# Two attention layers on a graph: one byte plane for two granules of the adjacency matrix, and one spill a block

## The reference, cut to what matters

```python
def layer0(h, adj, a):                       # N = 4096, D = 64
    src, dst = h @ a[:D, 0], h @ a[D:, 0]
    e = src[:, None] + dst[None, :]
    e = where(e > 0, e, 0.01 * e)
    e = where(adj > 0, e, -9e15)
    return softmax(e, axis=1) @ h
def layer1(x, adj, w, a, bias):
    wh = x @ w
    e = leaky_relu((wh @ a[:D, 0])[:, None] + (wh @ a[D:, 0])[None, :], 0.01)
    return softmax(where(adj > 0, e, -1e9), axis=1) @ wh + bias
x = layernorm(x + layer0(x, adj, a0))
x = layernorm(x + layer1(x, adj, w1, a1, bias1))
```

## Time and profile before

| | us |
|---|---|
| median of 3 runs | 499.06 (497.96 to 500.22) |
| the profiled execution | 498.63 |
| its span, first to last instruction | 496.9 |
| PE busy | 446.2 (90%) |
| PEld busy | 415.6 (84%) |
| DVE busy | 410.8 (83%) |
| ACT busy | 395.6 (80%) |
| POOL busy | 87.2 (18%) |
| VectorE, 32 x `to_bytes` | 74.1, 2315 ns each |
| HBM read / written | 77.74 MB / 9.44 MB |

### The profile page before, as it was taken

One profiled execution on the slowest core, in us unless ns is written; L12 is line 12 of the kernel. 1 busy time (PEld: TensorE's weight loads), 2 busy tenths in 40 slices (PEclk: granted clock), 3 DMA queues, 4 the chain that ended last, 5 costly groups with the idle time before them and its releaser, 6 DMA issues.

```text
span 496.9 us, 11765 instructions
## 1 busy us (share of the span) xinstructions
PE 446.2 (90%) x4420; PEld 415.6 (84%) x4420; DVE 410.8 (83%) x742; ACT 395.6 (80%) x589; POOL 87.2 (18%) x61
## 2 busy tenths in 40 slices
PE   0799768988989899998898969999999999999993
PEld 0379757978989799888887846999999999999993
DVE  3789999889899898998987897869496786968776
ACT  2695179778978979888792856999999999999940
POOL 0012221514214251241512220001010110101011
PEclk9987978997979979899997965999999999999998
DMA  7999999999999999999983100112020303031100
GB/s 194 252 242 280 261 268 292 334 302 319 318 321 321 293 337 309 321 324 311 342 257 129 44 0 2 46 41 66 32 71 24 95 0 95 0 95 37 58 12 13
DMA packets 80309, 87.68 MB, mean 176 GB/s; under 512 B 7314, under 2 KB 76178, under 8 KB 80274
## 3 DMA queue, kind: packets, MB, share of 16 engines
q1 hardware_dynamic: 45618, 52.98, 37.6%
q10 hardware_dynamic: 34656, 34.21, 25.0%
HBM read 77.74 MB, written 9.44 MB: 175 GB/s over the span
## 4 chain that ended last, share of the span: by engine, by line
PE 41%; DVE 24%; DMA 20%; issue 11%; POOL 1%; ACT 1%; SPq 1%; ACTq 0%; POOLq 0%; DVEq 0%
PE acc L434 37%; DMA stage<-in_adj 19%; DVE narrow L808 5%; DVE turned L820 3%; DVE pos L834 2%; DVE num L890 1%; PE flip L364 1%; DVE num L883 1%; DMA kept<-in_x 1%; DVE red L878 1%; DVE bn L895 1%; DVE kept L745 1%; PE acc L333 1%; DVE num L880 1%; DVE kept L742 1%
## 5 line engine op out<-in xcount | busy, mean ns | idle before, releaser
L574 ACT ACTIVATE neg<-srow,dcol 128x512 int8<-128x512 f32 (+1 forms) x320 | 221.7, 851 | 11.9 <-issue 7.0
L434 PE MATMUL acc<-xy_old,pos 128*128 128x195 bf16 x1024 | 197.6, 262 | 19.1 <-POOL pos L1025 11.9
L434 PE MATMUL acc<-xy_old,neg 128*128 128x195 bf16 x1024 | 197.3, 262 | 0.0
L434 PE MATMUL acc<-stage,pos 128*128 128x195 bf16 x1024 | 177.7, 248 | 0.0
L434 PE MATMUL acc<-stage,neg 128*128 128x195 bf16 x1024 | 177.6, 248 | 0.0
L574 ACT ACTIVATE neg<-xy_old,dcol 128x512 int8 x192 | 137.4, 850 | 0.0
L434 PEld LDWEIGHTS acc<-xy_old,pos 128*128 128x128 fp8e4 x1024 | 107.1, 105 | 28.0 <-issue 26.2
L434 PEld LDWEIGHTS acc<-xy_old,neg 128*128 128x128 fp8e4 x1024 | 106.3, 104 | 1.4
L434 PEld LDWEIGHTS acc<-stage,pos 128*128 128x128 fp8e4 x1024 | 100.8, 98 | 0.3
L434 PEld LDWEIGHTS acc<-stage,neg 128*128 128x128 fp8e4 x1024 | 100.3, 98 | 0.3 <-issue 0.3
L808 DVE TENSOR_SCALAR narrow<-stage 128x4096 uint8<-128x4096 int32 x32 | 74.1, 2315 | 14.5 <-DMA stage<-in_adj 13.5
(11 more groups left out here) (121 smaller groups left out, 331.9 us busy)
## 6 DMA issues: line engine op xcount, KB each, us to landing
stage<-in_adj ACTq DMA_DIRECT2D x64, 512.0 KB, 9.1
stage<-in_adj SPq DMA_DIRECT2D x64, 512.0 KB, 9.1
spill<-turned SPq DMA_DIRECT2D x16, 512.0 KB, 7.8
turned<-spill SPq DMA_DIRECT2D x16, 512.0 KB, 3.9
out<-x1s SPq DMA_DIRECT2D x7, 128.0 KB, 1.9
xn<-in_x SPq DMA_DIRECT2D x1, 768.0 KB, 16.8
kept<-in_x SPq DMA_DIRECT2D x4, 128.0 KB, 3.9
kept<-in_x ACTq DMA_DIRECT2D x4, 128.0 KB, 4.9
```

The lines of the kernel that those rows point to most:

```text
L434: last = nc.tensor.matmul(acc[:, r, c * XW:(c + 1) * XW], masks[c][:, t // BYTES, t % BYTES, r * P:(r + 1) * P], xy[layer][:, g * GT + t, ...
L574: last = nc.scalar.activation(o[:, t // BYTES, t % BYTES, :], row, ACT.Sign, bias=dcol[:, layer, col:col + 1])
```

## The change

Granule 3 gets another byte code: 0x40, which is 2.0 in fp8, where granules 0 to 2 keep 0x38, 1.0. The two codes have no set bit in common, so the planes of granules 2 and 3 can share one plane by a bitwise or. VectorE does that once a block (`join`), after the block's last mask of layer 0 and after the turn of the next block's granule 0. One plane per block is spilled, for blocks 0 to 6; block 7's stays in `turned[:, 0]`. SyncE issues the spill between its loads of granules 1 and 2, and waits for the join there. `turn` of granule 2 waits for that spill, `turn` of granule 3 for the join. Layer 1 takes the joined plane for both granules and picks the bits out with `& CODES[g]` inside its two mask instructions. The planes are reloaded one a block, alternately into a free part of the staging memory and into `turned[:, 1]`, a block or more ahead. The tables of granule 3 are halved in `split`, with two instructions in the place of one. Layer 1's loops on SyncE and VectorE become unrolled Python loops.

```diff
@@ -68,8 +68,9 @@
 
 
 
-    CODE = 0x38
-    CODES = 0x38383838
+    CODE = (0x38, 0x38, 0x38, 0x40)
+    CODES = (0x38383838, 0x38383838, 0x38383838, 0x40404040)
+    WORTH = (1.0, 1.0, 1.0, 2.0)
     FREE_AT_FIRST = RING * RB
     LINKS = 8
     HALVES = (slice(0, RB // 2), slice(RB // 2, RB))
@@ -83,7 +84,7 @@
         def sem(name):
             return ctx.enter_context(nc.semaphore(name))
 
-        spill = nc.dram_tensor("spill", (NS, NG - KEEP, P, GN), U8, kind="Internal").ap()
+        spill = nc.dram_tensor("spill", (NS - 1, P, GN), U8, kind="Internal").ap()
 
         kept = sb("kept", [P, NS * KEEP * GN], U8)
         stage = sb("stage", [P, SLOTS, GR * JC], I32)
@@ -184,8 +185,9 @@
         rows_kept = sem("rows_kept")
         narrowed = sem("narrowed")
         turned_ready = sem("turned_ready")
-        spilled = [sem(f"spilled{g}") for g in range(NG - KEEP)]
-        reloaded = [sem(f"reloaded{g}") for g in range(NG - KEEP)]
+        joined = sem("joined")
+        spilled = sem("spilled")
+        reloaded = [sem(f"reloaded{n}") for n in range(2)]
         signs_ready = sem("signs_ready")
         neg_ready = sem("neg_ready")
         pos_half = sem("pos_half")
@@ -212,6 +214,13 @@
         def xT_at(s):
             return xT[:, bass.ds(s * SUP, SUP)]
 
+        plane_even = stage[:, :, :].rearrange("p s n -> p (s n)").bitcast(U8)[:, 4 * XYW:4 * XYW + GN]
+
+        def plane_at(s):
+            if s == NS - 1:
+                return turned[:, 0, :]
+            return turned[:, 1, :] if s % 2 else plane_even
+
         def mask_at(s, g):
             if g < KEEP:
                 return kept[:, bass.ds(s * (KEEP * GN) + g * GN, GN)]
@@ -258,15 +267,13 @@
             sp.dma_start(wext1[0:D, 0:D], w1).then_inc(s_w, 16)
             sp.dma_start(wext1[D:E, 0:D], bias1.rearrange("(o d) -> o d", o=1)).then_inc(s_w, 16)
 
-            def spill_out(s, g):
-                sp.wait_ge(turned_ready, s * NG + g + 1)
+            def spill_out(s):
+                sp.wait_ge(joined, s + 1)
                 sp.sem_inc(sp_turn, 1)
-                sp.dma_start(spill[bass.ds(s, 1), g - KEEP].rearrange("o p n -> (o p) n"), turned[:, g - KEEP, :])\
-                  .then_inc(spilled[g - KEEP], 16)
-
-            def reload(s, g):
-                sp.dma_start(turned[:, g - KEEP, :], spill[bass.ds(s, 1), g - KEEP].rearrange("o p n -> (o p) n"))\
-                  .then_inc(reloaded[g - KEEP], 16)
+                sp.dma_start(spill[bass.ds(s, 1)].rearrange("o p n -> (o p) n"), turned[:, 0, :]).then_inc(spilled, 16)
+
+            def reload(s):
+                sp.dma_start(plane_at(s), spill[s]).then_inc(reloaded[s % 2], 16)
 
             for g in range(SLOTS, NG):
                 sp.wait_ge(narrowed, g - SLOTS + 1)
@@ -276,20 +283,18 @@
                     sp.wait_ge(narrowed, s * NG + g - SLOTS + 1)
                     sp.sem_inc(sp_turn, 1)
                     load(sp, LOWER, s, g)
-                    if g < NG - KEEP:
-                        spill_out(s - 1, KEEP + g)
-            for g in range(KEEP, NG):
-                spill_out(NS - 1, g)
-
-            for g in range(KEEP, NG):
-                sp.wait_ge(spilled[g - KEEP], 16 * NS)
-                sp.wait_ge(pos_ready, (NS - 1) * NG + g + 1)
-                reload(0, g)
-            with sp.Fori(1, NS) as s:
-                for g in range(KEEP, NG):
-                    sp.wait_ge(pos_ready, (NS + s - 1) * NG + g + 1)
-                    sp.sem_inc(sp_turn, 1)
-                    reload(s, g)
+                    if g == 1:
+                        spill_out(s - 1)
+            sp.wait_ge(spilled, 16 * (NS - 1))
+            sp.wait_ge(narrowed, NS * NG)
+            reload(0)
+            sp.wait_ge(joined, NS)
+            sp.wait_ge(pos_ready, NS * NG)
+            reload(1)
+            for s in range(1, NS):
+                if s + 1 < NS - 1:
+                    sp.wait_ge(pos_ready, (NS + s) * NG)
+                    reload(s + 1)
                 sp.wait_ge(x1_ready, NS + s + 1)
                 sp.sem_inc(sp_turn, 1)
                 sp.dma_start(rows_of(out, s - 1, RB, P), x1s[:, :, :]).then_inc(stored, 16)
@@ -739,8 +744,15 @@
                 t = slice(g * GT, (g + 1) * GT)
                 shape = (P, 2, GT, E)
                 hi, mid, lo = (xy[layer][:, t, :, part, :].rearrange("p t c f -> p c t f") for part in range(PARTS))
-                step(nc.vector.tensor_tensor(rest, wh[layer][:, t, :].unsqueeze(1).broadcast_to(shape),
-                                             wts[:, :, t].unsqueeze(3).broadcast_to(shape), ALU.mult))
+                if WORTH[g] == 1.0:
+                    step(nc.vector.tensor_tensor(rest, wh[layer][:, t, :].unsqueeze(1).broadcast_to(shape),
+                                                 wts[:, :, t].unsqueeze(3).broadcast_to(shape), ALU.mult))
+                else:
+                    for c in range(2):
+                        last = nc.vector.scalar_tensor_tensor(rest[:, c], wh[layer][:, t, :], 1.0 / WORTH[g],
+                                                              wts[:, c, t].unsqueeze(2).broadcast_to((P, GT, E)),
+                                                              ALU.mult, ALU.mult)
+                    step(last)
                 step(nc.vector.tensor_copy(hi, rest))
                 step(nc.vector.tensor_tensor(rest, rest, hi, ALU.subtract))
                 step(nc.vector.tensor_copy(mid, rest))
@@ -808,36 +820,56 @@
                 nc.vector.tensor_scalar(
                     narrow[:, 0:GN].rearrange("p (b g j) -> p g b j", b=GB, g=GR),
                     stage[:, g % SLOTS, :].rearrange("p (g b j) -> p g b j", g=GR, b=GB),
-                    0.0, float(CODE), ALU.is_gt, ALU.mult).then_inc(narrowed, 1)
+                    0.0, float(CODE[g]), ALU.is_gt, ALU.mult).then_inc(narrowed, 1)
 
             def turn(s, g):
 
                 k = s * NG + g
                 if g >= KEEP and s > 0:
-                    dve.wait_ge(pos_ready, k - NG + 1)
-                    dve.wait_ge(spilled[g - KEEP], 16 * s)
+                    dve.wait_ge(joined, s)
+                    if g == KEEP:
+                        dve.wait_ge(spilled, 16 * s)
+                    else:
+                        dve.wait_ge(pos_ready, k - NG + 1)
                 dve.wait_ge(narrowed, k + 1)
                 nc.vector.transpose(words(mask_at(s, g)), words(narrow[:, 0:GN])).then_inc(turned_ready, 1)
 
+            def join(s):
+
+                dve.wait_ge(pos_ready, s * NG + KEEP + 1)
+                dve.wait_ge(neg_ready, s * NG + NG)
+                nc.vector.tensor_tensor(words(turned[:, 0, :]), words(turned[:, 0, :]), words(turned[:, 1, :]),
+                                        ALU.bitwise_or).then_inc(joined, 1)
+
             def mask(layer, s, g):
                 k = (layer * NS + s) * NG + g
 
                 c = words(neg[:, g, :])
-                a = words(mask_at(s, g))
                 dve.wait_ge(signs_ready, k + 1)
                 if layer == 0:
+                    a = words(mask_at(s, g))
                     dve.wait_ge(turned_ready, s * NG + g + 1)
-                elif g >= KEEP:
-                    dve.wait_ge(reloaded[g - KEEP], 16 * (s + 1))
-                if layer == 0:
                     half = slice(GW // 2, GW)
-                    nc.vector.scalar_tensor_tensor(words(pos[:, g, :])[:, half], c[:, half], CODES, a[:, half],
+                    nc.vector.scalar_tensor_tensor(words(pos[:, g, :])[:, half], c[:, half], CODES[g], a[:, half],
                                                    ALU.bitwise_xor, ALU.bitwise_and).then_inc(pos_half, 1)
                     dve.wait_ge(pos_half, k + 1)
-                nc.vector.tensor_tensor(c, c, a, ALU.bitwise_and).then_inc(neg_ready, 1)
-                if layer == 1:
+                    nc.vector.tensor_tensor(c, c, a, ALU.bitwise_and).then_inc(neg_ready, 1)
+                elif g < KEEP:
+                    a = words(mask_at(s, g))
+                    nc.vector.tensor_tensor(c, c, a, ALU.bitwise_and).then_inc(neg_ready, 1)
                     dve.wait_ge(neg_ready, k + 1)
                     nc.vector.tensor_tensor(words(pos[:, g, :]), a, c, ALU.bitwise_xor).then_inc(pos_ready, 1)
+                else:
+                    a = words(plane_at(s))
+                    if s < NS - 1:
+                        dve.wait_ge(reloaded[s % 2], 16 * (s // 2 + 1))
+                    else:
+                        dve.wait_ge(joined, NS)
+                    nc.vector.scalar_tensor_tensor(c, a, CODES[g], c, ALU.bitwise_and, ALU.bitwise_and)\
+                      .then_inc(neg_ready, 1)
+                    dve.wait_ge(neg_ready, k + 1)
+                    nc.vector.scalar_tensor_tensor(words(pos[:, g, :]), a, CODES[g], c, ALU.bitwise_and, ALU.bitwise_xor)\
+                      .then_inc(pos_ready, 1)
 
             every = slice(0, RB)
 
@@ -923,6 +955,8 @@
```

(5 more changed lines are left out.)

## The result

| | before | after |
|---|---|---|
| median | 498.51 us (496.42 to 500.22, 4 runs) | 520.48 us (517.09 to 521.21, 4 runs) |
| ratio to before | | 1.0415, 95% interval 1.0374 to 1.0456 |
| span of the profiled execution | 496.9 us | 518.7 us |
| mean of the five middle bodies | 30.01 us | 33.23 us |

The kernel became 4.2% slower; 504.5 us was predicted, with 510 as the upper end. The sign was right, the size about four times too small: 5.4 us of loss forecast against 22.0 measured.

The account below looks back on a forecast made before the run. The prediction took PE to bound layer 1, and VectorE's sequence plus DMA waits to bound layer 0's bodies. Added VectorE work and a later granule 2, less old waits, gave +5.9 us on 498.63: 504.5 us, 8 in 10 range 496 to 510.

Parts of the forecast that it names:

- The bound of each stage: PE alone sets layer 1's time; a layer 0 body is 27.9 us of VectorE's sequence plus 2.1 us waiting for DMA.
- The split's two instructions: Granule 3's table split on VectorE takes 1.38 us instead of 1.21, adding 0.15 us once in layer 0.
- The join: The or of two planes adds 1.15 us a body on VectorE, raising its floor from 27.9 to 29.05 us.
- No wait before granule 1: In layer 0's bodies granule 1 lands about 1.3 us earlier, so VectorE's old 0.65 us wait for it goes.
- SyncE's queue: In layer 0 the spill waits for the or of the planes, so granule 2's lower half is issued 4.6 us late.
- From the last byte to VectorE's start: For granule 2's lower half in layer 0, about 0.4 us from the last byte to the semaphore.
- the new wait: VectorE's wait for granule 2's late lower half in layer 0: 1.5 to 1.8 us a body, taken as 1.7.
- That a single queue gets nearly the whole rate: One queue alone moves granule 2's halves in layer 0 at about 321 GB/s, judged from a reload at 287 GB/s.
- The first body: Layer 0's first body loses 0.6 us, with 0.25 us of waiting for granule 2, as DMA was less full.
- The sum: Five middle bodies +0.75 us each, first +0.6, last +1.4, table split +0.15: in all +5.9 us.
- C: Rival: a slow stretch makes granule 2's wait 2.7 us, 511 us; extreme, unused queue turns, 4.0 us, some 520; chance 0.10.
- A: Rival: DMA relief counts in full, no wait for granule 2, bodies of VectorE's 29.05 us, 494.0 us; chance 0.17.

## Why the prediction was wrong, by its steps

- **The bound of each stage** was right: all of the loss lies ahead of layer 1's long stretch, nearly all of it in layer 0's bodies. The split's two instructions and the waits around the last join moved nothing that can be seen.
- **The join** was to cost 1.15 us and costs 1.38; VectorE's sequence for a body is 33.23 less 4.05 of waiting, 29.18 us, where I had 29.05.
- **No wait before granule 1** holds in six of seven bodies (1.18 us in the last).
- **SyncE's queue.** The spill was to be issued 6.7 us into the body and is issued at 6.91, the lower half 0.7 us behind it. The order was right, and the lateness is 5.1 us where I had 4.6. This was the deciding step, as I had said.
- **From the last byte to VectorE's start: this is the term of the sum that failed.** I had 0.4 us; it is 2.90 in the mean of the five middle bodies, 3.8 in the one at 192.82 (207.5 to 211.27). It alone makes the new wait 4.05 us (3.0 to 4.7) instead of 1.7: by the count above the lower half's last bytes come at 14.9 us of the body, where I had 15.1, and VectorE is ready at 13.8, where I had 13.7. The 0.4 us fits a reload with nothing behind it, whose last packet starts at 316.89 and which has landed at 317.35. In layer 0 the trace of before already has 2.2 us ahead of the same narrowing. With that the prediction's own working gives a wait of about 3.5 us instead of 1.7.
- **"That a single queue gets nearly the whole rate" was wrong too, but its errors cancelled.** I took it from the reload of 316 to 317 us, 287 GB/s, but that is a transfer to all 128 partitions in 4 KB packets, and the loads write 32 at a time. The upper half takes about 5 us at some 205 GB/s where I had 3.3 us at 321, and the spill falls behind it. The lower half then takes 5.2 us alone at 205, where I had 5.9 us with 321 shared with granule 3's upper half, which doesn't start before 206.9 though issued at 202.01. The bytes so ended when I had said, by luck.
- **The first body** has 2.80 us of the new wait, not 0.25. That its DMA was less full (286 GB/s) bought nothing: there the last bytes come at 15.1 us too.
- **The sum.** Middle bodies +3.22 each instead of +0.75, 16.1 us; the first +3.08 instead of +0.6; from the start of the last to layer 1 +3.04 (68.53 to 71.57 us) instead of about +1.55. With 0.09 us ahead of the first that is the 22.3 us of the later start.
- **The rule I leant on.** The Trainium skill (DMA: Bandwidth & Descriptors, "Queues, rings and completion order") has each DMA engine alternate between the queues that have work. The side-by-side stretches fit that; the runs with loads issued ahead don't: there the other queue's transfer waited for them (2.6 to 6.0 us). And the turns that an empty queue leaves were no help to a load that writes one half of the partitions: 205 GB/s alone, 347 with both.
- **Rivals.** The extreme of C, a queue that can't use the other's turns, new wait 4.0 and some 520 us, is what came, to within half a microsecond, and by luck: its spill of 3.0 us and lower half of 6.5 us are both too long, and its 0.4 us to the landing is too short. I set it aside by the 287 GB/s, a misread row. Nor is its cause the one seen: a lone queue reaches 349 to 417 GB/s when it writes all partitions. A's 494.0 us, with VectorE alone as the limit, is what the same join gives (494.87) once its spill stands behind granule 2's load.
- **The range** ended at 510 since I capped the unknown at a wait of 2.7 us by the slowest stretch of before, 231 GB/s. That varied the rate and left the landing at 0.4 us, so the term that failed had no share in the range.

Still open: by which rule a transfer on the second queue is let in (with four ahead it starts beside the fourth, with three behind nearly all), and what the 2.2 to 3.8 us between a lower half's last bytes by the count and VectorE's start consist of. No run varied them by themselves. Ahead of the spill the same late half had 1.0 to 2.1 us, with its bytes no earlier (15.1 us of the body), so what stands behind a transfer may matter; that isn't shown.

## What to carry to other kernels

Take a transfer's rate, and its time from the last byte to the landing, from a row of the same kind: its partitions, its packet size, its queue, and what else is in flight. Where two queues fill two halves of the partitions, issue both halves at the same time: here 5.1 us of lateness in one queue cost 3.2 us in each body, and 5.7 us cost 4.1. So a spill or store that waits for anything belongs behind the loads that someone waits for. Before a change that saves DMA bytes, try the same kernel with the saved transfer only moved: here that alone was worth 1.7%, and the kernel with the saving stayed at 0.9%.

## What the runs showed of the hardware that I had not expected

- Loads to 32 partitions at a time move at 204 to 218 GB/s, whichever queue and whether in 1 KB or 4 KB runs; to 128 partitions at 349 (1 KB) and 417 (4 KB). Two queues, one on partitions 0 to 63 and one on 64 to 127, reach 347. On this last point the Trainium skill (SBUF — State Buffer, "Can I just issue two DMAs to hit both halves?") says that two such transfers serialize, with 6% gained; here it was 347 against 204 to 218, and the measurement decides.
- A load on an otherwise empty queue starts 2.6, 4.5, 5.8 and 6.0 us after its issue behind one, two, three and four loads of the other queue; with nothing ahead the first packet comes after 1.0 us (9.39 to 10.38).
- Between the last bytes of a granule, by the count, and VectorE's start lie 1.9 to 2.3 us before and 2.2 to 3.8 after in the middle bodies; a reload with nothing behind it lands about 0.5 us after its last packet starts.
- The packet share is 1.12 at 204 GB/s and 1.10 at 347: it tells that DMA has work, not its rate.
- GpSimd's two-input operation on 128x1024 words stretched VectorE's narrowing beside it from 2.29 to 3.7 to 4.1 us, or VectorE's half mask from 0.69 to 2.85.
